# A GRU scan with a mixture of experts beside it: two buffers for y, block work moved between ScalarE and GpSimd, the router earlier, the expert weights joined on VectorE

## The reference

```python
def cell(h, x):
    gi = x @ W_ih + b_ih
    gh = h @ W_hh + b_hh
    i_r, i_z, i_n = jnp.split(gi, 3, axis=-1)
    h_r, h_z, h_n = jnp.split(gh, 3, axis=-1)
    r = sigmoid(i_r + h_r);  z = sigmoid(i_z + h_z)
    n = tanh(i_n + r * h_n)
    return (1 - z) * n + z * h
# h: all states, [16 * 256, 512]
norm = maximum(l2_norm(h), 1e-12)
weights = softmax(h / norm @ router_w)          # 8 experts
rw, selected = top_k(weights, 2);  rw = rw / sum(rw)
combine = sum over the two of one_hot(selected) * rw
out = x + sum over e of combine[:, e] * (h @ Wa[e] @ Wb[e])
```

## Time and profile before

| | |
|---|---|
| time, median of 3 runs | 1135.05 us (1133.69 to 1135.05) |
| the profiled execution's own time | 1136.39 us |
| its span, first to last instruction | 1134.6 us |
| TensorE busy | 1011.4 us, 89% of the span |
| VectorE busy | 885.4 us, 78% |
| ScalarE busy | 713.1 us, 63% |
| GpSimd busy | 299.9 us, 26% |
| granted TensorE clock | 0.998 of full speed |

### The profile page before, as it was taken

How to read it: one execution, slowest core, us unless ns; L and a number is a source line. 1 busy time by engine, 2 the same in 40 slices (tenths; PEclk the granted TensorE clock), 3 DMA queues, 4 the chain that set the end, 5 groups by cost and what they waited for, 6 DMA issues and landing times. The chain is left out here.

```text
span 1134.6 us, 63208 instructions
## 1 busy us (share of the span) xinstructions
PE 1011.4 (89%) x30603; PEld 743.1 (65%) x21839; DVE 885.4 (78%) x3471; ACT 713.1 (63%) x2824; POOL 299.9 (26%) x762
## 2 busy tenths in 40 slices
PE   5678989998989999999999999999999999989996
PEld 3566666676666676666676666676666676666764
DVE  6878777778777788777788777788777788777886
ACT  6667665666665666665666665666665666665664
POOL 1032222322222322222322222322222322222223
PEclk9999999999999999999999999999999999999999
DMA  8220111111111011111011111011111011100000
GB/s 271 87 77 15 27 27 29 23 29 26 27 27 28 23 30 27 26 27 28 23 29 27 27 27 28 23 30 27 27 26 29 23 29 26 28 27 19 8 10 29
DMA packets 49509, 38.99 MB, mean 34 GB/s; under 512 B 34676, under 2 KB 39112, under 8 KB 49224
## 3 DMA queue, kind: packets, MB, share of 16 engines
q1 hardware_dynamic: 48376, 31.41, 10.4%
q10 hardware_dynamic: 848, 3.54, 0.9%
HBM read 18.94 MB, written 8.39 MB: 24 GB/s over the span
## 5 line engine op out<-in xcount | busy, mean ns | idle before, releaser
L460 POOL TENSOR_TENSOR y<-y 128x128 f16<-128x128 f32 x256 | 111.4, 435 | 470.5 <-ACT y L665 417.6
L972 PE MATMUL gates<-whh,st 128*32 128x256 f16 x4080 | 158.8, 274 | 68.4 <-DVE st L789 64.6
L864 PE MATMUL pairs<-wx,xs 128*32 128x256 f16 x4096 | 215.2, 273 | 0.0
L864 PE MATMUL ybank<-hparts,wa 128*128 128x128 f16 x2048 | 214.6, 220 | 0.1
L616 ACT ACTIVATE rr<-pre 128x64 f32<-128x64 f32 x256 | 65.6, 256 | 235.9 <-DVE pre L763 235.9
L864 PEld LDWEIGHTS ybank<-hparts,wa 128*128 128x128 f16 x2048 | 164.5, 98 | 40.7 <-issue 27.3
L855 PE MATMUL ybank<-hparts,wa 128*128 128x128 f16 x1024 | 185.0, 219 | 0.0
L972 PEld LDWEIGHTS gates<-whh,st 128*32 128x32 f16 x4080 | 90.8, 95 | 142.5 <-ACT gates L578 132.4
L977 PE MATMUL gates<-whh,hparts 128*32 128x256 f16 x4080 | 158.1, 273 | 0.0
L760 DVE STREAM_TRANSPOSE tr<-gates 128x256 f32<-128x256 f32 x256 | 114.8, 448 | 49.5 <-PE gates L977 49.1
L855 PE MATMUL pairs<-wx,xs 128*32 128x256 f16 x2048 | 148.5, 273 | 0.0
(11 more groups left out here) (145 smaller groups left out, 2101.5 us busy)
## 6 DMA issues: line engine op xcount, KB each, us to landing
out<-outb SPq DMA_DIRECT2D x63, 128.0 KB
xin<-in_x SPq DMA_DIRECT2D x58, 128.0 KB
wih<-in_L_cond_W_ih ACTq DMA_DIRECT2D x4, 768.0 KB, 7.5
whh<-in_L_cond_W_hh SPq DMA_DIRECT2D x4, 768.0 KB, 11.7
wih<-in_L_ffn_Wb SPq DMA_DIRECT2D x8, 256.0 KB, 3.1
xs<-xh SPq DMA_TRANSPOSE x116, 2.6
wih<-in_L_ffn_Wa SPq DMA_DIRECT2D x4, 256.0 KB, 5.1
whh<-in_L_ffn_Wa SPq DMA_DIRECT2D x4, 256.0 KB, 3.1
```

The lines of the kernel that those rows point to most:

```text
L460: nc.gpsimd.tensor_tensor(y[:, m % YB, 1, :], y32[:, :], y[:, m % YB, 0, :], ALU.subtract).then_inc(ylo_ready, 1)
L864: return nc.tensor.matmul(out, lhsT, rhs, start=start, stop=stop, skip_group_check=True)
L972: nc.tensor.matmul(gates[32 * j:32 * j + 32, 0:2 * P], st[:, k, :], whh[:, 1, k, j, 0:2 * P], start=False, stop=False, skip_group_check=True)
```

## The change

1. y32 gets two buffers, so ScalarE's float32 copy waits only for the subtraction of the expert before the last.
2. On ScalarE, splitting x moves from s = 5 to s = 6, scaling it from s = 7 to s = 2 of the next block. The gather of states leaves ScalarE and goes to GpSimd, both parts at s = 0; only the last block's stays on ScalarE. Reading the router's bank moves into `gru_step`, right behind the seeding for the next step.
3. On GpSimd, the two halves of x's low part move from s = 0 and 4 to s = 2 and 5; the inverse norm comes ahead of the two subtractions for y.
4. The router comes ahead of the experts' products in the wide step s = 3 and uses ybank1 instead of nbank (nbank for the last block); the odd expert's product at s = 3 waits until the bank is read.
5. The picks no longer hold the weights: they are made before these are there, scaled by a constant. When the weights come, GpSimd multiplies the second pick, and VectorE multiplies the first and adds (a new instruction ahead of the first expert's sum).
6. On VectorE, the transpose of z comes right behind the sum for r, and the sum for z moves behind r times h_n.
7. SyncE loads and stores x and out one step earlier in the block, and issues the low parts' transposes two steps later.

```diff
-        wts = sb("wts", [P, 2])
+        second = sb("second", [P, NE])
-        y32 = sb("y32", [P, P])
+        y32 = sb("y32", [P, 2, P])
+        def router_bank(f):
+            return ybanks[1] if f < NB - 1 else nbank
-        X_AT = 5
+        SPLIT_AT, SCALE_AT = 6, 2
...
# SyncE, beside(n)
-                    if s == 2:
+                    if s == 4:
                         sp.wait_ge(xlo_begun, b + 1 - FIRST)
                         turn_x(b, 1, 0)
-                    if s == 5:
+                    if s == 7:
                         sp.wait_ge(xlo_ready, b + 1)
                         turn_x(b, 1, 1)
-                if 1 <= i and i + 3 < NB and s in (3, 4):
-                    load_x(i + 3, s - 3)
-                if 2 <= i and s in (6, 7):
-                    store(i - 2, s - 6)
+                if 1 <= i and i + 3 < NB and s in (2, 3):
+                    load_x(i + 3, s - 2)
+                if 2 <= i and s in (5, 6):
+                    store(i - 2, s - 5)
...
# GpSimd
+            def gather_states(f, part):
+                pool.wait_ge(both_parts_ready, 2 * ((f + 1) * S + 1))
+                wait(pool, logits_done, f)
+                nc.gpsimd.tensor_copy(hf[:, part, :, :].rearrange("p k (s b) -> p (k s) b", b=B),
+                                      hparts[:, f % HB, :, :, part * B:(part + 1) * B].rearrange(
+                                          "p k s b -> p (k s) b")).then_inc(hf_ready, 1)
...
-                nc.gpsimd.tensor_tensor(y[:, m % YB, 1, :], y32[:, :], y[:, m % YB, 0, :], ALU.subtract
+                nc.gpsimd.tensor_tensor(y[:, m % YB, 1, :], y32[:, m % 2, :], y[:, m % YB, 0, :], ALU.subtract
...
# at the end of gaps(f)
+                pool.wait_ge(gap_ready, 3 * (f + 1))
+                wait(pool, comb_ready, f)
+                for t in range(2):
+                    nc.gpsimd.tensor_scalar(pick[:, t, :], expert_no[:, :], top_no[:, t:t + 1], 1 / PROD_SCALE,
+                                            ALU.is_equal, ALU.mult).then_inc(pick_ready, 1)
             def combine(f):
-                pool.wait_ge(wt_ready, f + 1)
-                nc.gpsimd.tensor_scalar(wts[:, :], wt[:, :], 1 / PROD_SCALE, None, ALU.mult).then_inc(comb_step, 1)
-                ...
-                for t in range(2):
-                    nc.gpsimd.tensor_scalar(pick[:, t, :], expert_no[:, :], top_no[:, t:t + 1], wts[:, t:t + 1],
-                                            ALU.is_equal, ALU.mult).then_inc(comb_step, 1)
-                ...
-                nc.gpsimd.tensor_tensor(comb[:, :], pick[:, 0, :], pick[:, 1, :], ALU.add).then_inc(comb_step, 1)
+                pool.wait_ge(pick_ready, 2 * (f + 1))
+                pool.wait_ge(wt_ready, f + 1)
+                wait(pool, comb_ready, f)
+                nc.gpsimd.tensor_scalar(second[:, :], pick[:, 1, :], wt[:, 1:2], None, ALU.mult
+                                        ).then_inc(second_ready, 1)
# GpSimd, beside(n)
-                if s in (0, 4) and 1 <= i and i + 2 < NB:
-                    split_x(i + 2, s // 4, n)
+                if s == 0 and 1 <= i:
+                    for part in range(2):
+                        gather_states(i - 1, part)
+                if s in (2, 5) and 1 <= i and i + 2 < NB:
+                    split_x(i + 2, s // 3, n)
+                if s == 3 and 1 <= i:
+                    invert_norm(i - 1)
                 if s % 2 and 0 <= n - DOWN:
                     low_y(n - DOWN)
                     low_y(n - DOWN + 1)
                 if s == 3 and 1 <= i:
-                    invert_norm(i - 1)
                     gaps(i - 1)
...
# ScalarE
+                if n % S == 3 and n >= S:           # in gru_step, behind seed and seed_z
+                    read_router(n // S - 1)
-                wait(act, ylo_ready, m)
-                nc.scalar.activation(y32[:, :], y_at(m)[:, 0:P], ACT.Copy, scale=1 / PART_SCALE).then_inc(y32_ready, 1)
+                wait(act, ylo_ready, m - 1)
+                nc.scalar.activation(y32[:, m % 2, :], y_at(m)[:, 0:P], ACT.Copy, scale=1 / PART_SCALE).then_inc(y32_ready, 1)
-                if s in (1, 2) and 1 <= i:
-                    gather_states(i - 1, s - 1)
-                if s == X_AT and i + 3 < NB:
+                if s == SPLIT_AT and i + 3 < NB:
                     split_x(i + 3)
-                if s == X_AT + 2 and i + 3 < NB:
-                    scale_x(i + 3)
+                if s == SCALE_AT and 1 <= i and i + 2 < NB:
+                    scale_x(i + 2)
...
# VectorE, gru_step(n), behind the sum for r
-                nc.vector.tensor_tensor(pre[:, HN, :, :], ...).then_inc(hn_summed, 1)
                 dve.wait_ge(z_done, n + 1)
                 nc.vector.transpose(tr[:, 2 * K:3 * K, :], zbank[:, 0:P]...).then_inc(z_turned, 1)
-                dve.wait_ge(z_turned, n + 1)
-                nc.vector.tensor_tensor(pre[:, ZG, :, :], ...).then_inc(z_summed, 1)
+                nc.vector.tensor_tensor(pre[:, HN, :, :], ...).then_inc(hn_summed, 1)
                 dve.wait_ge(hn_summed, n + 1)
                 dve.wait_ge(r_ready, n + 1)
                 nc.vector.tensor_tensor(rhn[:, :, :]..., rr[:, :], pre[:, HN, :, :]..., ALU.mult).then_inc(rhn_ready, 1)
+                dve.wait_ge(z_turned, n + 1)
+                nc.vector.tensor_tensor(pre[:, ZG, :, :], ...).then_inc(z_summed, 1)
# VectorE, add_expert(m)
-                if e == 0:
-                    dve.wait_ge(comb_step, (f + 1) * COMB_STEPS)
+                if e == 0:
+                    dve.wait_ge(second_ready, f + 1)
+                    nc.vector.scalar_tensor_tensor(out=comb[:, :], in0=pick[:, 0, :], scalar=wt[:, 0:1],
+                                                   in1=second[:, :], op0=ALU.mult, op1=ALU.add).then_inc(comb_ready, 1)
+                    dve.wait_ge(comb_ready, f + 1)
...
# TensorE, route(f)
-                wait(pe, acc_done, n - UP)
+                if f == NB - 1:
+                    pe.wait_ge(acc_done, LEFT - 1)
+                else:
+                    pe.wait_ge(yhi_ready, f * NE + 2)
+                    pe.wait_ge(y32_ready, f * NE + 2)
# TensorE, expert_down(m)
+                if e == 3 and f < NB - 1:
+                    pe.wait_ge(router_read, f + 1)
# TensorE, wide_step(n)
                 pair_ahead(n, (0,))
+                if s == 3 and 1 <= i:
+                    route(i - 1)
                 if 0 <= n - DOWN:
                     expert_down(n - DOWN)
                 if i + 1 < NB:
                     n_part(i + 1, s // 2, n)
-                if s == 3 and 1 <= i:
-                    route(i - 1, n)
                 if 0 <= n - DOWN:
                     expert_down(n - DOWN + 1)
```

More of the change, by code:

```diff
@@ L226, in gru_moe_kernel @@
         wt_ready = sem("wt_ready")
-        comb_step = sem("comb_step")
+        pick_ready = sem("pick_ready")
+        second_ready = sem("second_ready")
+        comb_ready = sem("comb_ready")
         y_done = sem("y_done")
@@ L241, in upper_half @@
             return sqs[:, part, :].bitcast(BF16).rearrange("p (c h) -> p c h", h=2)[:, :, 1]
-        SQ_STEPS, TOP_STEPS, RN_STEPS, COMB_STEPS = 4, 2, 2, 4
+        SQ_STEPS, TOP_STEPS, RN_STEPS = 4, 2, 2
         SPLITS = []
@@ L649, in read_router @@
                 wait(act, rnorm_step, f * RN_STEPS)
-                nc.scalar.activation(router[:, :], nbank[:, P:P + NE + 1], ACT.Copy).then_inc(router_read, 1)
+                nc.scalar.activation(router[:, :], router_bank(f)[:, P:P + NE + 1], ACT.Copy).then_inc(router_read, 1)
             def weigh(f):
@@ L654, in weigh @@
                 act.wait_ge(gap_ready, 3 * f + 2)
-                wait(act, comb_step, f * COMB_STEPS)
+                wait(act, comb_ready, f)
                 nc.scalar.activation(wt[:, :], gap[:, :], ACT.Sigmoid, scale=rnorm[:, :]).then_inc(wt_ready, 1)
@@ L776, in gru_step @@
                                         pre[:, HN, :, :].rearrange("p k b -> p (k b)"), ALU.mult).then_inc(rhn_ready, 1)
+                dve.wait_ge(z_turned, n + 1)
+                nc.vector.tensor_tensor(pre[:, ZG, :, :], tr[:, 2 * K:3 * K, 0:B], tr[:, 2 * K:3 * K, B:2 * B],
+                                        ALU.add).then_inc(z_summed, 1)
                 if n % S == 0:
@@ L924, in n_part @@
                         wait(pe, acc_done, n - UP)
-                    if b >= 2 and m == 2 and i == 0:
-                        pe.wait_ge(router_read, b - 1)
                     mm = product((pw, ph) == (0, 1), n_at(b, m)[:, 0:P], win[:, pw, k, m, :], turned(b, k, ph),
@@ L987, in state_part, with route @@
                 mm.then_inc(z_done, 1)
-            def route(f, n):
+            def route(f):
+                bank = router_bank(f)
                 if f == 0:
                     pe.wait_ge(weights_split, splits_before(N_RW_SPLITS))
-                wait(pe, acc_done, n - UP)
+                if f == NB - 1:
[3 more added lines that the diff above has]
+                    pe.wait_ge(y32_ready, f * NE + 2)
```

(8 more changed lines are left out.)

14 lines of the change are left out of this document (2 added, 12 removed).

## The result

The changed kernel takes 1088.51 us (median of 4, 1088.12 to 1089.09) against 1134.47 of the kernel before in the same runs: ratio 0.9596, 95% interval 0.9579 to 0.9612, 46 us less. I had forecast 1124 and a range down to 1097. The way was right, the size wasn't.

A forecast was written before the change was run, and what follows sets the result against it. Bound by a repeating recurrence, 3.79 us a step, with excesses in steps 2, 3 and 4. Terms sum to -0.39 us a block, times 29 -11.3; 1136.4 - 11.3 + 0.6 - 1.3 gives 1124, range 1097 to 1146.

The forecast's parts named there:

- What bounds the kernel: Whole loop: recurrence 3.79 us a step; step 4 waits for comb 2.44, step 2 for ScalarE's gather; TensorE fills step 3.
- Gather on GpSimd: Step 0: two copies hold VectorE's sums; cost 2A - 0.7 for copy A; at 0.85 us, 1.0 us.
- Order of the sums: VectorE, four even steps: z's sum moved later makes tanh start 0.08 us later in each.
- Blocks 1 and 2: Counted like all blocks 1 to 29, each at -0.39 us.
- y32 doubled: GpSimd's second subtraction follows at once: step 0 gains 0.10 us, step 2 loses 0.11, step 6 keeps 0.11.
- First half of x at step 2: GpSimd's queue delays the squares; TensorE waits 0.9 us, so step 3 grows from 4.26 to 5.16.
- Weights and picks: Step 4: shorter GpSimd queue before the weights cuts 6.11 us to 3.93, -2.18.
- Rival 1: Step 0: copies don't hold VectorE or are short enough to fit; 29 us more won, 1095; chance 0.15.
- Rival 2: Step 0: slow copies, slower than before from 1.03 us on; 1146 at 1.24 us; chance 0.20.
- rival 3: Step 3: squares come in time, TensorE doesn't lose 0.9 us; 26 us more won, 1098; chance 0.10.
- rival 4: Step 4: stall moves rather than goes, coefficients 0.3 to 0.4 us late a block; 1132 to 1135; chance 0.07.
- three signs: Prediction wrong if step 0 stays at 3.9, a copy takes over 1.03 us, or step 3 stays near 4.3.

The follow-up runs named there:

- before_split_behind: Kernel before, with only the second half of x's low part (step 4) moved behind the experts' weights in GpSimd's queue: 1089.87 us.
- gather_on_act: Changed kernel with the gather of states back on ScalarE, in steps 1 and 2: 1077.03 us.
- best_old_sums: Changed kernel with gather on ScalarE and router in its old place (1054.7 us), plus VectorE's old order of the sums: 1054.23 us.
- best_y32_one: Changed kernel with gather on ScalarE and router in its old place (1054.7 us), but one y32 buffer: 1080.65 us.
- squares_first: Changed kernel with both subtractions of the squares ahead of the split of x in GpSimd's queue: 1091.63 us.
- before_comb: Kernel before, with the split of x behind the weights and, of the change, only the fifth part (picks without weights): 1091.06 us.

## Why the prediction was wrong

*What bounds the kernel.* Right: the stall for comb in step 4, ScalarE's gather in step 2, TensorE full in step 3. before_split_behind shows the first.

*Gather on GpSimd.* This is the step that failed: "I take 0.85, near the middle". The mechanism and the formula held, the copy's length didn't. With the measured distance of 0.55 to 0.61 us the formula gives 0.4 to 0.5; gather_on_act measures 0.37 for it. I had counted 1.00, so 0.63 x 29 = 18 us of the 36 us that I was off. I took the middle between a write-only and a two-operand instruction; the copy of one operand lay at the write-only end (0.56).

*Order of the sums.* Wrong in sign. The delay of tanh that I worked out is there (0.06 to 0.09 us against my 0.08; the steps get 0.04 to 0.06 longer by it), but in three of the four even steps; what I left out is that the order also hides z's transpose behind GpSimd's holds. In the changed kernel the order gains 8 us where I had it cost 9; without the copies on GpSimd it makes no difference that can be told (best_old_sums). All that is left besides the gather in steps 0 to 2 and 4 to 7, this and smaller collisions, is 0.34 us of a block, some 10 us; the runs don't divide it further.

*Blocks 1 and 2.* I counted them like the others. They take 34.25 and 33.37 us after 38.88 and 35.23 (same distances), 6.5 us less together instead of 0.8; that is 3.5 us more than two common blocks are off. The stall of step 4 is not the reason: it gives 2.45 us in block 1 and 2.24 elsewhere. The surplus is in steps 2, 3 and 6 of block 1 (5.02 to 3.87, 5.84 to 5.33, 5.08 to 4.27). In step 2 of the kernel before, ScalarE had the wait for y32 (1.22 us), the gather and the split of a weight (0.63) ahead of r's sigmoid.

*y32 doubled.* I priced it by its collisions alone, at about nothing. The collision in step 0 was sized rightly (0.10 forecast, 0.11 in best_y32_one). With the gather on GpSimd the rest may be nothing too, which was not tried; with the gather on ScalarE the buffer is worth 26 us (best_y32_one). I had read ScalarE's wait for the subtraction, but not followed who is late behind it.

*First half of x at step 2.* Right: 5.00 against the forecast 5.16, TensorE stands 0.65 us for the squares. The difference is 0.16 x 29 = 5 us. Right too, but with nothing to spare, was that the read would be over in time: the odd product starts the moment it may (squares_first).

*Weights and picks.* Right as a whole: 3.88 against 3.93. I gave the credit in one lump; the runs split it: the split's move is 1.57 of 2.24 us and by itself equals the whole change.

*The rivals.* Rival 1 named 1095, nearest to 1088.5, yet its mechanism is refuted, and the nearness is luck: the copies do hold VectorE, and taking them away brings 11.5 us, not 29. The measured time is that low because several terms were off the same way. By the Trainium skill (SBUF — State Buffer, Who interferes with whom) a GpSimd instruction that reads SBUF and a VectorE instruction with two SBUF inputs block each other for the whole instruction; the timeline of step 0 agrees, with L772 and L777 at 0.40 us instead of 0.23 and 0.18, each ending 0.08 behind a copy. The 769 ns that the Trainium skill (GPSIMD Engine Reference, Performance versus the Vector engine) states for 512 elements is above the 0.61 measured. Rival 2 needed a copy of 1.03 us, rival 3 a step 3 without TensorE's wait, rival 4 a wait for the weights in step 4: none is there (the wait for the second pick is 2.7 us in the whole run, once). None of the three signs that I had named as showing me wrong came either; I had set one for a copy too slow and none for a copy too fast.

So the change is 80 us of gain and 34 us given back: without the gather on GpSimd and without the router's move it takes 1054.7 us, 80 below the kernel before (1134.5) and 34 below the changed one (1088.5). What was given back lies in two steps: step 0, for the copies, and step 3, for the squares.

## What to carry to other kernels

Read the queue of the engine that the stall names, in order, before rearranging anything: here one instruction with a wait of its own stood ahead of what was urgent, and moving it alone was as good as the whole change. When work goes to GpSimd, ask when it runs beside VectorE's two-operand instructions; the same copies cost 11 us at one time and nothing 2.8 us later. An instruction moved behind the urgent one can still hold VectorE there, as the split does in before_comb. And when a product is moved ahead, count both ends: what it needs then, and who must wait until its bank is read.

## What the runs showed that I had not expected

A held VectorE instruction holds up those behind it that GpSimd alone would not hold: with the old order z's transpose starts at 554.61, exactly when the copy ends. The hold lasts as long as the GpSimd instruction, however small the VectorE one is: comb, of 128x8, takes 0.52 us beside a split of x and 0.23 alone. A GpSimd copy of 128x512 float16, reading 16 of every 32 columns, follows another at 0.55 us, a fifth less than the 0.68 us of a two-operand subtraction of half as many columns.
